# Attention passes of a graph network: TensorE makes the queries of slot k+1 ahead of the sums of slot k, and two engines' loops are written out

## The reference

```
q, k, v = h@Wq+bq, h@Wk+bk, h@Wv+bv            # 4 heads of 32
alpha   = sum_c q[tgt] * (k[src] + w*We) / sqrt(32)   # per edge and head
a       = softmax of alpha over the edges of each target
out     = segment_sum((v[src] + w*We) * a, tgt)
h       = relu(batchnorm(gate(out, h@Wskip+bskip))) + h
```

## Time and profile before

| what | value |
|---|---|
| timed runs | 11557.31 us median of 3 (11550.38 to 11558.18) |
| profiled execution, first to last instruction | 11449.9 us |
| timed median less profiled span | 107.4 us |
| busy, share of span: TensorE / VectorE / ScalarE / GpSimd | 45% / 33% / 21% / 58% |
| mean granted TensorE clock, share of full | 0.641 |
| moved by transfers | 131 GB/s over the span |

### The profile page before, as it was taken

One profiled execution on the slowest core, in us unless ns is written; L12 is line 12 of the kernel. 1 busy time (PEld: TensorE's weight loads), 2 busy tenths in 40 slices (PEclk: granted clock), 3 DMA queues, 4 the chain that ended last, 5 costly groups with the idle time before them and its releaser, 6 DMA issues. The chain is left out here.

```text
span 11449.9 us, 117522 instructions
## 1 busy us (share of the span) xinstructions
PE 5176.2 (45%) x24082; PEld 4506.4 (39%) x24083; DVE 3769.5 (33%) x11072; ACT 2381.4 (21%) x4785; POOL 6613.1 (58%) x6804
## 2 busy tenths in 40 slices
PE   1333333335333333335555555555645555555556
PEld 1332323334323333334444444444444444444444
DVE  3000000001000000005555555555755555555557
ACT  3333333332000000004222222222212222222222
POOL 4655555563666666664555555555535555555555
PEclk6555555557566655667666666666776666666667
DMA  4222222225333333334555555555345555555553
GB/s 138 87 92 93 92 89 87 94 101 173 95 96 101 97 99 97 100 103 151 161 161 162 160 161 160 160 158 165 99 154 160 164 160 157 165 159 160 158 162 109
DMA packets 732493, 1500.95 MB, mean 131 GB/s; under 512 B 196632, under 2 KB 380039, under 8 KB 712059
## 3 DMA queue, kind: packets, MB, share of 16 engines
q0 software_dynamic: 260288, 643.14, 18.6%
q10 hardware_dynamic: 208064, 480.72, 12.4%
q1 hardware_dynamic: 263674, 371.92, 10.5%
HBM read 1282.90 MB, written 212.30 MB: 131 GB/s over the span
## 5 line engine op out<-in xcount | busy, mean ns | idle before, releaser
L1536 POOL DMA_INDIRECT conv_kv<-key_value,conv_src x3320 | 3284.5, 989 | 2458.6 <-issue 950.6
L795 POOL DMA_INDIRECT first_msg<-sage_in,first_src x1564 | 1479.2, 946 | 1053.0 <-SPq L756 579.5
L795 POOL DMA_INDIRECT second_msg<-sage_hidden_projected,second_src x1564 | 1479.1, 946 | 1003.3 <-issue 452.7
L1778 PE MATMUL conv_ps_sums<-conv_kv,conv_sel 128*128 128x136 f32 x6640 | 1437.0, 382 | 1089.0 <-DVE sums L1690 975.9
L1778 PEld LDWEIGHTS conv_ps_sums<-conv_kv,conv_sel 128*128 128x128 f32 x6640 | 1286.3, 277 | 1198.8 <-issue 709.1
L927 PE MATMUL first_ps_sums<-first_msg,first_sel 128*128 x3328 | 830.6, 428 | 1587.1 <-ACTq L821 855.9
L1764 PE MATMUL conv_ps_query<-query_table,conv_selT 128*128 x6640 | 1438.8, 384 | 172.4 <-issue 171.9
L1863 ACT ACTIVATE conv_selT<-conv_place,minus_partition 128x512 f32<-128x512 f32 x830 | 598.2, 721 | 4060.9 <-PE conv_ps_query L1764 1426.2
L927 PEld LDWEIGHTS first_ps_sums<-first_msg,first_sel 128*128 128x128 f32 x3328 | 718.0, 318 | 1711.3 <-issue 1711.3
L1764 PEld LDWEIGHTS conv_ps_query<-query_table,conv_selT 128*128 128x128 f32 x6640 | 1277.8, 283 | 241.5 <-issue 218.4
L1690 DVE TENSOR_TENSOR sums<-sums,conv_ps_sums 128x136 f32 x3320 | 972.1, 293 | 1179.8 <-remote 516.7
(11 more groups left out here) (267 smaller groups left out, 4369.7 us busy)
## 6 DMA issues: line engine op xcount, KB each, us to landing
conv_place<-place_rows SPq DMA_DIRECT2D x416, 512.0 KB
conv_sel<-selections ACTq DMA_DIRECT2D x830, 256.0 KB
selections<-first_sel ACTq DMA_DIRECT2D x52, 2048.0 KB
second_sel<-selections ACTq DMA_DIRECT2D x104, 1024.0 KB
conv_kv<-key_value,conv_src POOLq DMA_INDIRECT x3320
first_msg<-sage_in,first_src POOLq DMA_INDIRECT x1564
second_msg<-sage_hidden_projected,second_src POOLq DMA_INDIRECT x1564
conv_pen<-run_penalties SPq DMA_DIRECT2D x416, 48.5 KB
```

The lines of the kernel that those rows point to most:

```text
L795: pool.indirect_dma_start(msg[:, j * MW:j * MW + D], None, table, bass.IndirectOffsetOnAxis(ap=src[:, b, j:j + 1], axis=0)).then_inc(gathe ...
L1536: pool.indirect_dma_start(kv[:, h * CH + j, :], None, t.kv_d, bass.IndirectOffsetOnAxis(ap=src[:, h, j:j + 1], axis=0)).then_inc(gathered[ ...
L1778: last = pe.matmul(sums_of(h, step), sel[:, k % SELG, step % GR, :], kv[:, h * CH + step, DEN:2 * D], start=True, stop=True)
```

## The change

TensorE's list in a stage changes in the part with sums. Slot 3's queries stay where they were; from there on, each block of sums has the queries of the next slot ahead of it and not its own, and the last block of sums has the next chunk's slot 0 ahead of it. VectorE's list is the same. GpSimd's and ScalarE's loops become Python loops, so that every chunk's instructions stand in the program, with constants where the loop's register was.

```
@@ GpSimd
-                with pool.Fori(0, PAIRS - 1) as g:
+                for g in range(PAIRS):
                     for h in range(2):
                         gathers(chunk(g, h))
-                for h in range(2):
-                    gathers(chunk(PAIRS - 1, h))
@@ TensorE, stages(a, b, following)
                     pe.matmul(psFac, node[:, :], facm[:, :], start=True, stop=True).then_inc(expo_turned, 1)
+                    if a is not None:
+                        queries(a, NEAR, at)
                     for k, _, _, pairs in slots_of(a, b):
-                        if a is not None:
-                            if k == KG // 2:
+                        if a is not None and k + 1 < groups(a):
+                            if k + 1 == KG // 2:
                                 at = blocks_of(a, 1)
-                            queries(a, k, at)
+                            queries(a, k + 1, at)
+                        elif following is not None:
+                            queries(following, 0, blocks_of(following, 0))
                         sums(b, *pairs)
-                    if following is not None:
-                        queries(following, 0, blocks_of(following, 0))
@@ ScalarE
-                with act.Fori(0, PAIRS - 2) as g:
+                for g in range(PAIRS - 2):
                     stages(chunk(g + 1, 0), chunk(g, 1), chunk(g + 1, 1))
                     stages(chunk(g + 1, 1), chunk(g + 1, 0), chunk(g + 2, 0))
```

## The result

| | before | after |
|---|---|---|
| median, us (runs) | 11553.84 (4: 11538.30 to 11558.18) | 11654.76 (4: 11627.04 to 11685.47) |
| ratio | | 1.0093 [1.0073, 1.0114] |
| profiled execution, span | 11449.9 | 11624.8 |
| stages with gathers, mean of 98, us, traces | 54.00 | 55.37 |
| of these 56.5 us or longer | 2 | 20 |

The 98 stages are the 2nd to the 50th of each pass: the first, a start-up stage of about 57 us, and those at the end of a pass, which have no gathers, are left out.

The account below looks back on a forecast made before the run. It took a closed chain of GpSimd's gather rows and late releases to bound each 53.88 us stage; 11449.9 us span + 307 us (3.07 in 50 stages of two passes) + 107.4 = 11864 us, 2.7% slower; range 11300 to 11980.

Parts of the forecast that it names:

- (a): Slot 4's queries and block load now precede the stage's first sums: 3.07 us later, delaying GpSimd's first gather; 307 us.
- (b) to (d): Queries of slots 4, 5 and 7 ready earlier: VectorE's waits 1.62, 5.52, 4.60 us go or move to sums; gain 0.
- rival 3: Faster: VectorE's waits at L1562 are real and go, 10.6 us over 100 stages, 1060 us, giving 10500 us; chance 0.10.
- second link of the chain: In each stage, 2.83 us from TensorE's first sums until GpSimd resumes on the sums of steps 0 to 3.
- less than 2 us later: Sign on a stage's first sums: if they start less than 2 us later, step (a) is wrong.
- lower bound of 1.4: Least delay of the first sums, slot 4's queries at full clock and 0.53 idle: 1.4 us a stage, 11697 us.
- All at once: After about six gathers in a row, TensorE's finished work becomes known late, together, some 2 us after the row ends.
- (f): ScalarE's selections and transfers are let go earlier; it is busy 11.3 of 53.9 us, nobody waits long: 0.
- (g): GpSimd's and ScalarE's loops written out: taken as 0; gain at most 15 us, loss at most 133 us.
- bound of 133 us: Loss if written-out code had to be waited for once a stage, as long as the first gather's surplus (2.28 - 0.95 us).
- The 107.4 us: Gap between the timed median 11557.3 us and the profiled span 11449.9 us, added at the end of the sum.
- Rival 1: Not slower: GpSimd's later start is taken from its 7.46 us pause before the first gather; 11487 to 11557 us; chance 0.18.

Follow-up runs that it names:

- e_order: Only TensorE's list reordered against the kernel before, GpSimd's and ScalarE's loops both kept; 11591.61 us against 11449.52, ratio 1.0115.
- e_pool: Only GpSimd's loop written out against the kernel before, TensorE's old order and ScalarE's loop kept; 11444.18 us, ratio 0.9997.
- x_place: Kernel before with GpSimd's program written out, plus waits for the gather's own landing after gathers 20 and 26 of each chunk; 11047.98 us against 11444.95, ratio 0.965.
- x_start: Kernel before with GpSimd's program written out, plus landing waits after every sixth gather in a pass's first pair of chunks only; 11386.14 us, ratio 0.9948.
- x_half: Kernel before with GpSimd's program written out, two gathers a slot instead of four from the second pair of chunks on; 10126.48 us against 11442.94, ratio 0.8845.
- e_act: Only ScalarE's loop written out against the kernel before, TensorE's old order and GpSimd's loop kept; 11560.36 us, ratio 1.0087.

## Why the order costs anything: late sums or partial releases

**e_order_late4**: the new order, but slot 4's queries come behind the sums of steps 0 to 3, for which GpSimd's first gather waits.

```
+                        if a is not None and k == NEAR:
+                            sums(b, pairs[0], 2)
+                            pairs = (2, pairs[1])
```

> TensorE's new order with one exception: the sums of steps 0 to 3 stay ahead of slot 4's queries and its load of block numbers, so GpSimd's first gather is released as early as before; both loops stay. Theory (the order costs what it does because of these first sums): the median stage is back at 53.9 us (new order alone 55.1), ratio 1.000 to 1.005; the stages of 57 us and more become rare again if they come from the later rows. Rival (the queries of the next chunk ahead of the last sums, or the order of slots 5 to 7, cost): 1.008 to 1.012 as with the whole order.

1.0088 [1.0071, 1.0105], against 1.0115 [1.0091, 1.0139] for e_order: ordinary stages have 54.23 us, and 21 are long. Taking the forecast's own term (a) away returns about 0.3%, which the overlapping intervals don't make certain, and leaves 0.9%. By the traces of the two, (a) is worth 26 us in ordinary stages and ten long stages. So the later sums were the smaller part of the order's loss; the larger part is in long stages and what the order of the later slots adds.

If partial releases make long stages, a kernel in which GpSimd can't go on until TensorE's whole stage is known has none. The edit for that, called "drain" in the labels: slot 6's gathers, with which the third row starts, wait for all sums of chunk b and for the last queries of the stage.

```
-                        pool.wait_ge(sums_ready, KP * c + 2 * k + 2)
+                        pool.wait_ge(sums_ready, KP * c + (KP if k == 6 else 2 * k + 2))
+                        if k == 6:
+                            pool.wait_ge(q_ready, KG * c + 1 + SELG)
```

It adds conditions to a wait and removes none.

| kernel (base + drain) | ratio | mean, others | long | pause of row 3 |
|---|---|---|---|---|
| e_act_drain | 0.9967 [0.9954, 0.998] | 53.85 | 0 | 3.19 |
| after_drain | 0.9888 [0.9872, 0.9904] | 52.88 | 1 | 3.14 |
| before_drain | 0.998 [0.9972, 0.9989] | 54.58 | 0 | |
| order_drain | 0.9979 [0.997, 0.9987] | 54.46 | 2 | |
| pool_drain | 0.9964 [0.9948, 0.9979] | 53.96 | 0 | |
| pool_order_drain | 0.9905 [0.9887, 0.9922] | 53.19 | 1 | |

(before_drain and order_drain ran on the slower chip, where before has 11554.02 us, so their stages are compared with each other only. The other four ran where it has 11442 to 11445.)

> ScalarE's loop written out as in the run that was 1.0087, and one wait of GpSimd made stricter: ahead of a chunk's seventh slot of gathers it waits for the last sums of the stage and the next chunk's first queries, not only for the sums that free the places. Theory of the long stages: 26 of 98 stages there took 57 us and more, and nearly all follow a pause of GpSimd of 2.3 or 1.6 us in place of 3.0, in which only the first of TensorE's finished groups became known before gathers went on; with the stricter wait all are known first: long stages fall to a few, ratio 1.000 to 1.002. Rival (the long stages come from ScalarE's own code, fetched late): they stay, 1.007 to 1.010.

> The changed kernel with the same stricter wait of GpSimd. Theory: its 20 long stages of 98 go, the median stage of 54.7 us stays, so 0.8 us for 100 stages against the kernel before: ratio 1.005 to 1.008 in place of 1.009. Rival: the long stages belong to the new order itself (the next chunk's queries ahead of the last sums) and stay: 1.009 to 1.012.

e_act_drain takes ScalarE's written-out program from 1.0087 to 0.9967 and its long stages from 26 to none, with ordinary stages unchanged (53.83 and 53.85). One added wait removes just the long ones: that shows that they come of GpSimd's going on before TensorE's stage is known. What in the hardware then holds the rest back is not shown. The 0.3% below 1 lie mostly between the passes (328 us in place of 346). after_drain did better than either theory gave: it is 1.1% faster than before, on a chip of the faster kind. (after without the drain was timed on the slower kind only, so the step from 1.0093 to 0.9888 is across chips.) Its table row and GpSimd in one stage, from 6215.25 to 6268.32:

```profile
6215.20:6268.30 53.10, 28.83 (x138) 25.79 (x138) 29.30 (x92) 11.11 (x18) 30.39 (x33) 0.63 0.54 163
```

```profile
6214.38 0.94 POOL L1538 DMA_INDIRECT conv_kv<-key_value,conv_src  x1 [3.15 <-remote]
...
6231.83 0.94 POOL L1538 DMA_INDIRECT conv_kv<-key_value,conv_src  x1 [7.65 <-issue]
...
6249.58 0.94 POOL L1538 DMA_INDIRECT conv_kv<-key_value,conv_src  x1 [3.06 <-remote]
...
6267.45 0.94 POOL L1538 DMA_INDIRECT conv_kv<-key_value,conv_src  x1 [3.17 <-remote]
```

Its account is 40.0 + 7.35 + 2.76 + 2.87 = 53.0. The third row starts 0.87 us ahead of the next stage's start, in before 2.26 us: VectorE gets step 26's sum at 49.2 us behind the stage's start (before 50.9, after 51.4), and the next softmax starts sooner against the row.

**before_drain, order_drain, pool_drain, pool_order_drain**: the same drain, with the old and the new order, first with both loops kept and then with GpSimd's written out.

> The kernel before with only GpSimd's wait ahead of a chunk's seventh slot made stricter (all sums of the stage and the next chunk's first queries). Theory: in the kernel before nearly all pauses were already long enough for everything to become known, so it changes little in a stage; the same with ScalarE's loop written out gave 0.9967, most of it in the part between the passes: 0.996 to 1.000. Rival (the wait delays GpSimd): above 1.002.

> TensorE's new order with the same stricter wait, both loops kept. Theory (the order is a gain by itself; alone it costs because GpSimd goes on when only the first of TensorE's finished sums is known, and the rest is then held): as the changed kernel with this wait, 0.987 to 0.991, stages of 52.9 us. Rival (the order costs 1% by the later first sums, and the written-out loops gave the gain): 1.004 or more, stages of 54.5 us and more.

> GpSimd written out and its stricter wait, TensorE's order as before, ScalarE's loop kept. If the gain of 1.1% is the written-out GpSimd's with the wait, whatever the order: 0.987 to 0.991. If it needs the new order or ScalarE's written-out program: 0.996 to 0.999, as before_drain.

> The same with TensorE's new order. If the gain is that of the new order together with a written-out GpSimd: 0.987 to 0.991 here and 0.996 to 0.999 in the run with the old order; the last sums are then known early (first addition of the last slot at 49 us of the stage, as in the changed kernel with the wait, not at 51.5). If it needs ScalarE's program: 0.996 to 0.999 here too.

With the loops kept the order is free: 0.998 and 0.9979, where without the drain it cost 1.15% (on another chip). The long stages of the new order go too: of 31 and 20 in e_order and after there are 2, 1 and 1 left in order_drain, pool_order_drain and after_drain. With GpSimd's program written out it gains 0.6% (0.9964 and 0.9905, intervals apart; step 26's sum at 49.9). So in both pairs the new order costs nothing once GpSimd waits for the whole stage. Why it gains in one pair only stays open, and there are two rivals: GpSimd's straight program, which by itself changed nothing (e_pool), and the chip, since the pair with loops ran on the slower one and the pair without on a faster one. No run parts them.

**x_best, x_best_order**: x_place and x_start together, with the old and with the new order, on the slower chip.

> The two breaks a chunk (after gathers 20 and 26) and, in the first pair of chunks, a break after every sixth gather. Theory: the two gains add, 0.965 and 0.9948: 0.958 to 0.962. Rival (the pass's start sets how the rows lie against the stages, and they lie worse): 0.965 or more.

> The same with TensorE's new order. By the theory that the order is a gain by itself: queries are never what VectorE waits for and the last sums are known after gather 20's break, 0.95 to 0.958. By the reckoning of the prediction (the first sums of a stage 1.6 us later, and GpSimd has no slack left in this kernel to take it): 0.965 to 0.975.

0.9654 [0.9634, 0.9673] and 0.964 [0.9625, 0.9656]: the two don't differ by more than their intervals, and neither ratio is better than that of x_place alone (0.965, on a faster chip). The start rule shortened the stretch between the passes to 282 and 285 us (x_place has 334), but three and two stages with means of 71 and 76 us gave much of it back. x_place, two lines on the kernel before with GpSimd's program written out, is the simplest of the three and the version to keep.

## Why the prediction was right or wrong

- **Direction and place: right.** The waits of L1562 moved to the sums and gave nothing ((b) to (d)): 500 us there became 41, and the sums' remote waits rose from 244 to 753. Releases stayed 2 to 2.5 us behind a row's end, and stage 50 got no longer. x_half shows that gathers pace the stage. This is what ruled out rival 3, which the list of waits alone would have favoured.
- **The step that failed: (a), "3.07 us go into the second link of the chain", 307 us.** It was mis-sized twice. The first sums came 1.7 us later and not 3.07; by the prediction's own sign, "less than 2 us later", that makes (a) wrong. The step had 0.20 us of overlap and 0.94 of block load in it, and neither shows (16 matmuls in one row, no idle time); slot 4's group took 3.68 - 1.93 = 1.75 us. The lower bound of 1.4 was nearer. Then most of even that was covered. Before, the first gather ran beside VectorE's weighing (until about 16.3 us behind the start) and took 2.28 us; started behind it, it takes 0.94. Medians over the ordinary stages of e_order: first gather at 16.6 us in place of 14.9, and the second, a gather and a gap later, at 17.9 in place of 17.5. The prediction had both durations in the earlier trace rows and used 2.28 only to bound another part. An ordinary stage of e_order lost 0.58 us, 57 us in the two passes, where 307 stood in the sum.
- **What the sum lacked: long stages.** "All at once" was the premise, and by the pauses it held for 96 of 98 stages of the trace. In two it did not, and they were 58 us long; the prediction took stages for alike and never asked what the odd two were. The order, and ScalarE's written-out program, turn 18 to 34 more stages into such: about 106 us in e_order and 83 between the traces of before and after. That the total loss (101 us) is a third of the forecast, and has its sign, is so in part luck: a term that was not in the sum is the larger part of e_order's loss.
- **(f) and (g): GpSimd's half right, ScalarE's wrong.** "ScalarE is busy 11.3 of 53.9 us and nobody waits long for it: 0" is an argument from cover. It priced ScalarE's speed, and not that writing its loop out could bring long stages. Alone that costs 0.87%, within the bound of 133 us but by another mechanism: e_act_drain takes it away. How the written-out program shifts ScalarE's work was not read.
- **The 107.4 us** are a difference between chips. Added to a sum that is held against timed runs on the slower chip they belong there, and they leave the change of +307 us as it is; measured was +101.
- **The range.** The text gives 11957 as the upper end "with the bounds of (a) and the loss of (g)", but 11957 is (a) at 4 us alone; with the 133 us of (g) it would be 12090. It made no difference: the result lies below the range.
- Rival 1 (a later start of GpSimd costs nothing) was wrong as a mechanism, since ordinary stages of e_order did get longer. It came nearer in size, because most of the later start was covered.

## What to carry to other kernels

Where many indirect gathers are issued in a row, read TensorE's results as arriving when the row ends, and close a stage's time by the issuing engine's own account (gathers, pauses, surplus) before believing a list of waits. Look at the spread of the stages too: a rare long one in the profile of before is a mechanism that an edit may make common. Then choose where the row breaks: two waits for a landed gather, put where the small latency-bound answers are needed, gave 3.5%, and with one added wait for everything this change has a gain of 1.1% where it had a loss of 0.9% (on two chips).

## What the runs showed of the hardware that was not expected

- TensorE's finished work reaches VectorE and GpSimd late while GpSimd issues indirect transfers in a row: by up to 8.9 us in before, 5.2 in the long stage of e_act, and little with half the gathers. What holds it, the signals or the writes into PSUM, no run here tells; nor whether it is GpSimd's issuing or the gathers still on their way (the release comes 2.1 to 2.5 us behind the last issue, the landing in x_place 2.8 us behind it); nor why the pause behind a row comes in steps of about 1.6, 2.3 and 3.0 us.
- A first gather beside VectorE's 128x512 multiplies of two on-chip operands (L1590, seven without a gap) takes 2.28 us, and 0.94 without them. In 98 stages each of before, e_order and after_drain it ends about 0.82 us behind the end of the last multiply, wherever it starts, and takes 0.94 us when it starts behind that end. The Trainium skill ("GPSIMD Engine Reference", Key points) has GpSimd share its interfaces with VectorE where an instruction has two such operands; the trace agrees. Only one gather pays, 1.3 us, since it is held until the row of multiplies is over.
- Adding a wait can be worth more than removing one: x_half apart, which leaves work out, every kernel here that beats before has waits added.
- One kernel differs by 1% between chips (11443 and 11554 us). At this size only ratios taken on one chip mean anything, and stages of traces from two chips don't: ordinary stages have 54.58 us in before_drain on the slower chip and 53.96 in pool_drain on a faster one, which differ otherwise in a loop that alone cost nothing.
